# The recurrence's state decays, spread over the partitions through HBM

## What is computed

```python
def step(S, t):                      # S: per head a 128 x 128 state
    q_t, k_t, v_t, a_t, b_t = t
    y = jnp.einsum('bhvk,bhk->bhv', S, k_t)
    err = y - v_t
    S = a_t[..., None] * S - (b_t[..., None] * err)[..., None] * k_t[:, :, None, :]
    o = jnp.einsum('bhvk,bhk->bhv', S, q_t)
    return (S, o)
```

## Time and profile before

| | us |
|---|---|
| median of 3 runs | 3097.45 |
| lowest and highest run | 3096.15, 3103.75 |
| span of the profiled execution | 3102.6 |
| projection, up to the first load of the recurrence | 0 to 614 |
| recurrence, 32 chunks of 63 to 67 us | 614 to 2760 |
| feed-forward, the rest | to 3102.6 |

### The profile page before, as it was taken

The page is one execution under the profiler, slowest core; times in us unless marked ns, Lnnn a source line. Parts: engine busy times, 40 slices in busy tenths (PEclk is TensorE's granted clock), DMA queues, the critical chain, the costliest instruction groups (busy, mean ns, idle before and its releaser), DMA issues. The chain is left out here.

```text
span 3102.6 us, 48417 instructions
## 1 busy us (share of the span) xinstructions
PE 2732.2 (88%) x14144; PEld 1863.5 (60%) x14144; DVE 2239.8 (72%) x4680; ACT 1610.3 (52%) x3516; POOL 1377.8 (44%) x1760
## 2 busy tenths in 40 slices
PE   7999999768898888988889888898888888859999
PEld 3555555446666666666666666666666666635555
DVE  6777777677888878888788887888887888623332
ACT  6666666545555555555555555555555555412111
POOL 3666676734544445444454444544445444310000
PEclk9999999989999999999999999999999999979999
DMA  3655556533232232322323223232223222034120
GB/s 124 241 225 206 233 230 239 196 82 67 43 57 42 44 65 47 57 42 43 64 49 57 42 44 59 53 57 42 44 51 61 46 53 43 9 107 109 45 38 14
DMA packets 449883, 261.22 MB, mean 84 GB/s; under 512 B 402672, under 2 KB 414672, under 8 KB 447472
## 3 DMA queue, kind: packets, MB, share of 16 engines
q1 hardware_dynamic: 449664, 258.51, 31.5%
HBM read 153.42 MB, written 105.05 MB: 83 GB/s over the span
## 5 line engine op out<-in xcount | busy, mean ns | idle before, releaser
L265 DVE SCALAR_TENSOR_TENSOR A_acc<-A_psY,A_w,A_acc 128x410 f32<-128x410 f32 (+1 forms) x720 | 419.2, 637 | 151.6 <-ACT A_acc L334 151.6
L405 PE MATMUL A_psY<-A_xT,A_w 128*128 128x413 f32 (+1 forms) x960 | 347.2, 510 | 9.1 <-PE A_psAG L411 7.7
L1244 ACT ACTIVATE B_PQ<-B_psM 128x64 f32<-128x64 f32 (+2 forms) x480 | 125.2, 261 | 441.2 <-DVE B_NC L1137 440.9
L1137 DVE TENSOR_TENSOR B_NC<-B_NC,B_psM 128x256 f32<-128x256 f32 x480 | 200.8, 418 | 182.5 <-PE B_psM L1756 92.8
L192 POOL TENSOR_TENSOR A_outs<-A_outs,A_acc 128x410 f32<-128x410 f32 (+1 forms) x240 | 229.7, 987 | 216.1 <-ACT A_outs L342 216.1
L899 POOL TENSOR_TENSOR B_WT<-B_WT,B_G 128x128 f32<-128x128 f32 (+2 forms) x224 | 143.4, 640 | 371.2 <-ACT B_WT L1244 184.3
L1244 ACT ACTIVATE B_WL<-B_psT 64x128 f32<-64x128 f32 (+3 forms) x480 | 148.5, 309 | 265.6 <-PE B_psT L1723 265.4
L405 PEld LDWEIGHTS A_psY<-A_xT,A_w 128*128 128x128 f32 x960 | 180.2, 189 | 165.5 <-issue 164.2
L1140 DVE TENSOR_REDUCE B_W<-B_NC 128x64 f32<-128x320 f32 x512 | 248.7, 486 | 17.6
L334 ACT ACTIVATE A_acc<-A_psY,A_w 128x410 f32<-128x410 f32 (+1 forms) x240 | 166.1, 692 | 162.9 <-PE A_psY L405 161.2
L879 POOL TENSOR_TENSOR B_PQ<-B_PQ,B_G 128x256 f32<-128x256 f32 x128 | 89.4, 699 | 345.5 <-DVE B_WT L1105 345.5
(11 more groups left out here) (207 smaller groups left out, 6588.4 us busy)
## 6 DMA issues: line engine op xcount, KB each, us to landing
B_KQ<-scr SPq DMA_DIRECT2D x96, 512.0 KB, 6.6
scr<-A_outs SPq DMA_DIRECT2D x48, 615.0 KB, 3.5
scr<-A_outag SPq DMA_DIRECT2D x32, 615.0 KB, 5.2
scr<-A_outs SPq DMA_DIRECT2D x48, 409.0 KB, 2.5
A_xc<-nbeta SPq DMA_DIRECT2D x16, 1024.0 KB, 5.9
B_A<-scr SPq DMA_DIRECT2D x32, 512.0 KB, 4.6
B_C<-scr SPq DMA_DIRECT2D x32, 512.0 KB, 6.3
B_G<-scr SPq DMA_DIRECT2D x32, 512.0 KB, 4.6
```

The source lines that it names most:

```text
L265: nc.vector.scalar_tensor_tensor(a, y, w[:, s, col:col + 1], a, ALU.mult, ALU.add)\
L405: last = nc.tensor.matmul(psY[p][:, y0:y0 + HALO + t1 - t0], wp[:, p, kt, :], xT[:, kt, t0:t1 + HALO], start=kt == 0, stop=kt == KT - 1)
L1137: tt(eq[:, :, :, 1:5], eq[:, :, :, 1:5], left.unsqueeze(2).to_broadcast([128, H, R, R]), ALU.mult)\
L1244: copy = lambda out, in_: nc.scalar.activation(out, in_, ACT.Copy)
```

## The change

The "decay" jobs leave PE's tables. SP instead stores `Gs[4]` to a scratch tensor `decay` of 16 x 128 in HBM, in an order that makes each four-byte element a piece of its own, then loads all 2048 values on every partition with one broadcast (8 KB for each of 128 partitions). The target is the first eight rows of `WX`, which are free between `centered_copy` at j = 8 and `decayed_w` at the chunk's end. `decay_state` reads from there, and its first two calls move one step later, to j = 11 and j = 12. `block_decays` now waits for the store, `decayed_w` and `w_rows_copy` for all four calls of `decay_state`. In the projection, three semaphores that told SP that a weight buffer is free become one with three counts.

```diff
@@ project_inputs
-        w_used = [Count(sem(f"A_w_used{s}"), 1, 1, 1) for s in range(2)]
-        c_used = [Count(sem(f"A_c_used{s}"), 1, 1, 1) for s in range(2)]
-        ca_used = [Count(sem(f"A_ca_used{s}"), 1, 1, 1) for s in range(2)]
+        w_used = [Count(sem(f"A_w_used{s}"), 3) for s in range(2)]
...
-                    sp.wait_ge(w_used[s].sem, w_used[s].at(t, 1))
-                    sp.wait_ge(c_used[s].sem, c_used[s].at(t, 1))
-                    sp.wait_ge(ca_used[s].sem, ca_used[s].at(t, 1))
+                    sp.wait_ge(w_used[s].sem, w_used[s].at(t, 3))
...
@@ leaf_jobs
-        7: [("decay", 0)] + ([("oc_rest", 1)] if out else []),
+        7: ([("oc_rest", 1)] if out else []),
...
-        13: [("decay", 2), ("decay", 3)],
...
@@ recurrence
+        decay_d = nc.dram_tensor("decay", (H, D), FP32).ap()
...
+        dst, dld = Count(sem("decays_st"), 1, 16), Count(sem("decays_ld"), 1, 16)
...
+        WXF = WX[:].rearrange("p k x -> p (k x)")[:, 0:H * D]
+        GB = WXF.rearrange("p (h v) -> p h v", h=H)
...
+            def store_decays(g):
+
+                wait(sp, g4, g, 1)
+                wait(sp, dld, g, 0)
+                sp.dma_start(decay_d.rearrange("h v -> v h"), Gs[4][:].rearrange("p h j -> p (h j)"), allow_slow_non_contiguous=True)\
+                  .then_inc(dst.sem, 16)
+
+            def load_decays(g):
+
+                wait(sp, dst, g + 1, 0)
+                wait(sp, oc, g, 0)
+                sp.dma_start(WXF, decay_d.rearrange("h v -> (h v)").partition_broadcast(128)).then_inc(dld.sem, 16)
+
             for g in range(NCH):
                 at, n = (g + 1) * C, (g + 1) % 2
+                store_decays(g)
...
                     load("C0", n, at)
+                load_decays(g)
                 if g % 2 and g >= 3:
                     store((g - 3) // 2)
...
@@ block_decays
-                wait(pool, stg, g, 0)
+                wait(pool, dst, g, 0)
...
@@ decayed_w
+                wait(pool, stg, o + 1, 0)
...
             def decay_state(g, i):
                 wait(dve, cont, g, 4)
-                ps = take_bank(dve, g, "decay", i)
+                wait(dve, dld, g, 1)
                 x = ST[:, 4 * i:4 * i + 4, :]
-                tt(x, x, ps[:].rearrange("p (h v) -> p h v", h=4), ALU.mult).then_inc(stg.sem, 1)
+                tt(x, x, GB[:, 4 * i:4 * i + 4, :], ALU.mult).then_inc(stg.sem, 1)
...
@@ w_rows_copy
+                wait(act, stg, o + 1, 0)
```

More of the change, by code:

```diff
@@ L246, in _ @@
                 tap[p].start(dve)
-            c_used[0].start(dve)
-            c_used[1].start(dve)
             with dve.Fori(0, TURNS) as t:
@@ L268, in _ @@
                     dve.wait_ge(tap[2].sem, tap[2].at(t, 3 * (s + 1) * NTA))
-                    dve.sem_inc(c_used[s].sem, 1)
+                    dve.sem_inc(w_used[s].sem, 1)
         @block.scalar
@@ L315, in _ @@
             nc.scalar.activation(nbeta[:], beta[:], ACT.Copy, scale=-SCALE * SCALE).then_inc(nbeta_sb, 1)
-            for c in (*ag_free, *ca_used):
+            for c in ag_free:
                 c.start(act)
@@ L355, in _ @@
                     act.wait_ge(ag_free[0].sem, ag_free[0].at(t, (s + 1) * NTA))
-                    act.sem_inc(ca_used[s].sem, 1)
+                    act.sem_inc(w_used[s].sem, 1)
         @block.tensor
@@ L390, in _ @@
             pe.wait_ge(beta_sb, T // 512)
-            w_used[0].start(pe)
-            w_used[1].start(pe)
             with pe.Fori(0, TURNS) as t:
@@ L443, in leaf_jobs @@
         6: ([("oc", 1)] if out else []),
-        7: [("decay", 0)] + ([("oc_rest", 1)] if out else []),
+        7: ([("oc_rest", 1)] if out else []),
         8: ([("own", 0, 1)] if not last else []),
-        9: [("decay", 1)],
         10: ([("kk", 0, 0), ("kk", 0, 1)] if not last else []) + ([("var", 0)] if out else []),
@@ L647, in taken @@
                 return (am if n else atc, (g - 3) // 2, 1),
-            return {"contact": (cont, g, n + 1), "ktok": (ktok, g, n + 1), "decay": (stg, g, n + 1),
+            return {"contact": (cont, g, n + 1), "ktok": (ktok, g, n + 1),
                     "update": (stu, g, n + 1), "oc": (oc, g - 1, n + 1),
@@ L757, in _ @@
                 loaded(sp, what, NCH - 1)
+            wait(sp, dst, NCH, 0)
+            wait(sp, dld, NCH, 0)
             wait(sp, ldc, NCH, 0)
@@ L1186, in chunk @@
                     elif j == 10:
-                        decay_state(g, 0)
                         mask_gram(g, 5)
                     elif j == 11:
-                        decay_state(g, 1)
+                        decay_state(g, 0)
                         if more:
@@ L1194, in chunk @@
                     elif j == 12:
+                        decay_state(g, 1)
                         if more:
@@ L1595, in shared_job @@
                         last = nc.tensor.transpose(ps[:, 128 * m:128 * (m + 1)], KQ[:, s, 0, 2 * i:2 * i + 2, :].rearrange("p h c -> p (h c)"), ident[:])
[L1596 to L1600, removed]
                 elif kind == "oc":
```

## The result

| | before | after |
|---|---|---|
| median of four runs, us | 3098.11 | 3181.36 |
| lowest and highest, us | 3096.15, 3103.75 | 3169.07, 3188.90 |
| span of the profiled execution, us | 3102.6 | 3178.9 |
| mean granted clock | 0.976 | 0.954 |

The changed kernel takes 1.0261 times as long (interval 1.0236 to 1.0287), 83 us more. The direction was forecast, the size was not: 3126 us, with a range that ended at 3146.

The account below looks back on a forecast made before the run. Neither PE nor DVE was full; whichever wait ends last at each place was taken to set the time. The terms 0 + 13 + 16 + 0 = +29 us on 3097.45 gave 3126 us, range 3103 to 3146.

Parts of the forecast that it names:

- Part 1: PE: the 16 transposes leaving it stand in idle time, so removing them gains 0 us; bound 67 us.
- Part 2: DVE: decay_state moves later and reads SBUF, delaying the solve of j = 13; +13 us, bounds 6 and 21.
- Part 3: PE's clock: with less work around idle stretches it falls to half more often; +16 us, bounds 0 and 32.
- the second place, behind leaf 9: PE's idle stretch after the four transposes of j = 9: three clock falls at 1.12 us each, +3 us.
- The first piece: PE's idle stretch after j = 13: a clock fall in nearly every even chunk, nine more at 1.37 us, +12 us.
- Part 4: The two DMAs: broadcast load covered by 1.8 us, store bounded by 2 and 12 us with 3.4 us free; 0 us.
- late data: Rival: load lands over 8.5 us after issue, or store holds the queue over 3.4 us longer; 3150 or more, chance 0.12.
- The range: Whole kernel: measured time expected within 3103 to 3146 us, leaving out about 2 in 10.
- The signs I named: PE idle 2.5 us or more before j = 14's transpose, L1035 about 1.1 us, no DVE wait for DMA at j = 11.

Follow-up runs that it names:

- c1_behind_dummies: Changed kernel with the four-byte store issued behind the four loads and the 16 transposes kept on PE with no reader; 3107.4 us, 1.0031 of the kernel before.
- a3_dummies: Changed kernel with the 16 decay transposes back on PE at their old places, into banks nobody reads; 3119.7 us, 1.0066 of the kernel before.
- a1_store_behind: Changed kernel with the store of the decays issued behind the next chunk's four loads (K, KB, Q, A); 3161.3 us, 1.0200 of the kernel before.
- b1_store_only: Kernel before with the four-byte store added ahead of the loads, read by nobody, and the projection's merged counts; 3123.3 us, 1.0077 of the kernel before.

## Why the prediction was wrong

The steps between c1_behind_dummies, a3_dummies and the changed kernel give the terms of the real sum: place and operand 8 us, store 3119.7 - 3107.4 = 12, clock 3181.4 - 3119.7 = 62; together 82 of the 83 us. In the other order (through a1_store_behind) the clock is 54 and the store 20, so the two overlap by some 8 us. The store added alone to the kernel before cost 22 (b1_store_only); why it is only 12 with the rest of the change is open.

- **Part 1 (0): right in what it said, incomplete.** The transposes stood in idle time and gave nothing back: clean odd chunks take 66.2 us without them (a1_store_behind) and 66.1 with them (c1_behind_dummies). But that idle time was not harmless: see part 3.
- **Part 2 (+13): right within its bounds of 6 and 21.** Measured 8 to 10 us. The mechanism is the one described, with L1035 at 1.09 us and the lost wait. The term was 16 times 0.8; leaf 12 grew by 0.6, clean even chunks of c1_behind_dummies lose 63.7 - 63.0 = 0.7, and odd ones nothing. Of the 8 us the place accounts for 4; the other 4 are open.
- **Part 3 (+16): the step that failed, and most of the miss.** The mechanism was right, the size off by a factor of 3 to 4. The term that was mis-sized is the second place, behind leaf 9: +3 us in the prediction, about 34 measured.

  The first piece came as said. "I expect the fall in nearly every even chunk": all 15 even chunks from 2 on have a late one, as forecast.

  The second did not. "The stretch behind the four transposes of j = 9 becomes a second such place; I give it three falls at 64.05 - 62.93 = 1.12 us": there were ten. Four of its terms failed there. No row of before showed a fall in that place, so its number, three, came from nothing. I priced it by a short fall elsewhere, while these last 6.8 us. I wrote "Odd chunks have "wo" work there", which holds from j = 11 to j = 14 but not behind leaf 9, and five of the ten are in odd chunks. And I left the idle time there unworked: it grew from 0.68 to 1.11 us.

  The price of the ten, from a1_store_behind, where nothing else disturbs an odd chunk: its five odd chunks with a middle fall take 69.6 us on average, against 66.2 without, 3.4 us each; so ten cost some 34 (an estimate, as is the next). The late ones last 6.1 us on average, not 4.3. Even chunks of a1_store_behind with late falls alone take 65.0 us, against 63.7 clean in c1_behind_dummies, 1.3 each, 19 for fifteen, of which c1_behind_dummies pays 3 itself. That makes 34 + 16 = 50 of the 54 to 62.
- **Part 4 (0): the second step that failed.** The load was covered. The store was not: "I bound it by 2 and 12 us and take that of K", and K with 2048 pieces of 256 bytes was no neighbour of 2048 pieces of 4 bytes that are written to HBM. The store itself landed after 11.6 us in a1_store_behind, the bad end of my bound. The rival "late data" had its condition right (over 3.4 us of delay: POOL starts on A 5.1 us later), and at 0.12 too small a chance. The Trainium skill, DMA: Bandwidth & Descriptors, Rules for kernel authors, says that a non-contiguous last dimension becomes one descriptor per element and should be rearranged. The runs agree: the changed kernel moved 66560 more DMA packets under 512 bytes than the kernel before (469232 against 402672), where 32 stores of 2048 elements make 65536. 64-byte pieces in the same place let K, KB and Q land in 6.5 us, not 14.0.
- **The range** ended at +48 us, less than the upper bounds of parts 2 and 3 together (21 + 32 = 53), and held nothing for part 4. Its 32 assumed at most 12 more middle falls at a short fall's price. With place and operand at 8 us, the store's 12 to 20 and the clock's 50, the sum is 70 to 78, all of it beyond the range.
- **The signs I named** were right in kind: PE idles 2.40 us before the transpose of j = 14 (I said 2.5), L1035 takes 1.09, no DVE row of the recurrence waits for a DMA. None of them looked at the loads of A or at the odd chunks, where the sum failed.

## What to carry to other kernels

Before you take work off TensorE, ask what its clock does in each idle stretch that grows, in every kind of chunk and not just where it falls today: here 16 transposes that cost nothing in time were worth 54 to 62 us as work. Price a fall by its own place and length: a middle stretch of 6.8 us cost this loop 3.4 us, a late fall 1.3 on average. And a small DMA is priced by its pieces and by the loads that queue behind it: its own issue row shows nothing.

## What the runs showed of the hardware

- TensorE's stretches at half clock mostly lasted 3.4 or 6.8 us here; nine of all those counted, in six of the sixteen profiles, lasted 10.2 or 13.7. A 6.8 us stretch in the middle of an odd chunk cost 3.4 us (a1_store_behind).
- 2048 pieces of 4 bytes stored to HBM made the next three loads of 512 KB land after 14.0 us (median) instead of 6.6, while the store's issue took 0.38 us. 128 pieces of 64 bytes did not (6.5 us), and landed after 1.4 us themselves where the four-byte store took 11.6.
- A VectorE product of 128x512 fp32 took 1.024 us with one SBUF input read at a stride of 64 bytes, and 0.685 with both at stride one. The Trainium skill, SBUF — State Buffer, Door 1: The DMA port swizzle, says that SBUF is read in lines of 16 bytes and that a stride which meets a new line at each element is slower; the runs agree, half as long again.
